# A fused transformer block: another order of work inside the two narrow attentions

## The reference, cut to what matters

```python
x = x + _L0_xattn_ref(_layernorm(x), ctx, ctx, ...)        # "a"
y = _layernorm(x)
# the second layer, "m":
x1 = rmsnorm(y, norm1_w)
q = x1 @ Wq.T
latent = layernorm(x1 @ Wdkv.T, ln_g, ln_b)                # 64 wide
k = latent @ Wuk.T
v = latent @ Wuv.T
q = apply_rope(q)
k = apply_rope(k)
scores = einsum('bhqd,bhkd->bhqk', q, k) / sqrt(8)         # causal
attn = softmax(where(causal, scores, -inf))
y = y + (attn @ v) @ Wo.T
```

## Time and profile before

| | us |
|---|---|
| median of three runs | 2048.15 (2042.94 to 2048.78) |
| the profiled execution's own time | 2049.34 |
| its span | 2047.5 |
| first attention, steady part (66 to 424 us) | 358 |
| second attention, steady part (470 to 986 us) | 516 |
| PE busy over the span | 1493.7 (73%) |
| DVE busy | 1348.0 (66%) |
| ACT busy | 1172.9 (57%) |
| POOL busy | 773.1 (38%) |

### The profile page before, as it was taken

The page is one execution under the profiler, slowest core; times in us unless marked ns, Lnnn a source line. Parts: engine busy times, 40 slices in busy tenths (PEclk is TensorE's granted clock), DMA queues, the critical chain, the costliest instruction groups (busy, mean ns, idle before and its releaser), DMA issues. The chain is left out here.

```text
span 2047.5 us, 63292 instructions
## 1 busy us (share of the span) xinstructions
PE 1493.7 (73%) x22193; PEld 1111.0 (54%) x22194; DVE 1348.0 (66%) x3733; ACT 1172.9 (57%) x2974; POOL 773.1 (38%) x823
## 2 busy tenths in 40 slices
PE   0688888846888877788424992888888884499991
PEld 0466666624555555556223780566666663377781
DVE  4577777636777777776454664678777875366665
ACT  2366666623544444444433990798888883377770
POOL 0000000022322323231485561336666666466661
PEclk9999999967999999999556995899999996699996
DMA  7110000000001000000012223000011111222227
GB/s 231 32 34 27 31 31 25 26 6 27 31 20 33 21 29 25 26 33 18 23 43 72 74 66 96 12 12 30 29 32 32 31 36 33 79 81 77 81 77 250
DMA packets 110889, 100.81 MB, mean 49 GB/s; under 512 B 17827, under 2 KB 98598, under 8 KB 110656
## 3 DMA queue, kind: packets, MB, share of 16 engines
q1 hardware_dynamic: 87648, 67.02, 11.0%
q0 software_dynamic: 12928, 25.60, 3.8%
q10 hardware_dynamic: 10080, 5.01, 0.8%
HBM read 43.25 MB, written 32.96 MB: 37 GB/s over the span
## 5 line engine op out<-in xcount | busy, mean ns | idle before, releaser
L2497 POOL DMA_INDIRECT e_back<-e_out_rows,e_G x142 | 148.4, 1045 | 98.8 <-issue 56.7
L664 DVE TENSOR_REDUCE m_mx<-m_pM 128x8 f32<-128x1024 f32 x128 | 155.6, 1216 | 29.6 <-PE m_pM L375 29.5
L1459 ACT ACTIVATE w_weights<-w_pS,w_ng 128x77 f32<-128x77 f32 x512 | 157.8, 339 | 17.7 <-DVE w_ng L1547 17.5
L526 ACT ACTIVATE m_PT<-m_pS 128x1024 f32<-128x1024 f32 x128 | 130.4, 1019 | 59.3 <-PE m_pS L404 58.0
L1112 POOL DMA_INDIRECT e_rows<-re_R,re_index x128 | 126.1, 985 | 63.7 <-issue 35.2
L526 ACT ACTIVATE a_PT<-a_pS 77x1024 f32<-77x1024 f32 x128 | 130.5, 1019 | 17.8 <-PE a_pS L404 12.6
L2520 DVE TENSOR_TENSOR e_gl<-e_g,e_gh 128x512 f16<-128x512 f32 x142 | 98.3, 692 | 57.4 <-ACT e_g L2464 53.7
L769 POOL TENSOR_SCALAR a_var<-a_aggr 128x4 f32<-128x4 f32 x16 | 3.1, 193 | 337.0 <-DVE a_aggr L590 337.0
L1660 POOL TENSOR_TENSOR w_weights<-w_weights,w_rec 128x616 f32<-128x616 f32 x64 | 77.9, 1217 | 125.4 <-DVE w_rec L1551 125.0
L664 DVE TENSOR_REDUCE a_mx<-a_pM 128x8 f32<-128x616 f32 x128 | 101.5, 793 | 33.0 <-PE a_pM L375 33.0
L1459 ACT ACTIVATION_READ_ACCUMULATOR w_weights<-w_pS,w_ng 128x1 f32 x512 | 113.6, 222 | 0.0
(11 more groups left out here) (383 smaller groups left out, 5651.1 us busy)
## 6 DMA issues: line engine op xcount, KB each, us to landing
e_G<-e_rows SPq DMA_DIRECT2D x106, 132.0 KB, 2.3
e_B<-e_back SPq DMA_DIRECT2D x16, 512.0 KB, 6.9
stage<-in_split SPq DMA_DIRECT2D x13, 512.0 KB, 4.6
Qs<-a_qh SPq DMA_DIRECT2D x128, 32.0 KB
Qs<-m_qh SPq DMA_DIRECT2D x128, 32.0 KB
Ks<-m_kh SPq DMA_DIRECT2D x32, 128.0 KB
e_R<-e_back SPq DMA_DIRECT2D x16, 256.0 KB, 3.5
w_stage<-in_late SPq DMA_DIRECT2D x16, 256.0 KB, 2.6
```

What stands on the lines that cost most here:

```text
L526: act.activation(PT[:NK, b % 2, 8 * half:8 * half + 8, :], pS[:NK, :, :], ACT.Exp, scale=float(1.0 / np.sqrt(HD))).then_inc(exp_done, 1)
L664: dve.tensor_reduce(out=mx[:, 8 * half:8 * half + 8], in_=pM[:, :, :NK], op=ALU.max, axis=AX.X).then_inc(m_max, 1)
L1459: ac = act.activation(weights[:, b % 2, n, :], pS[:, n // HB, n % HB, :KC], ACT.Exp, bias=ng[:, b % 2, n:n + 1], scale=float(WD) ** -0.5, ...
L2497: pool.indirect_dma_start(out=back, out_offset=bass.IndirectOffsetOnAxis(ap=G[:, r, s, D:D + 1].bitcast(I32), axis=0), in_=out_rows[:, r, ...
```

## The change

It moves instructions and hands some to another engine. No product, sum or copy is added or taken away, except that the high half of the latents is now made from PSUM and not from the copy in SBUF.

- `max_transpose` and `keep_max` of sequence b + 1 stand in the second half of step b, before `scores` of the second half. They stood at the start of step b + 1.
- The second half of the maxima stands right behind the first half of the scores, ahead of `project_output` and `values`.
- On DVE the maximum of the first half comes first in a step, ahead of the part in the slot.
- latT is made in slot 0 of step 0 for the next group. It was made in slot 1 of step 3 for the group after the next. q moves to a third slot (2) in the middle of step 0. ACT makes both of latT's outputs, `lh` and `lt`.
- The normalised latents (`latents`) are written behind the second maximum of step 3.
- The high half of the rotated q is made in step 1 and that of k in step 2, behind `output_hi`. They were made at the end of steps 0 and 1.
- The four scaled rows of the RMS norm (`rms_rows`) are made by ACT, ahead of the first `exps` of step 2. DVE made them.
- POOL makes the root for the squares ahead of ks in step 1.

```diff
-            order = ["q", "qs", "k", "ks", "v", "x", "lat", "latT"]
+            order = ["latT", "q", "qs", "k", "ks", "v", "x", "lat"]
...
-            slots = {(0, 0): "q", (0, 1): "qs", (1, 0): "k", (1, 1): "ks", (2, 0): "v", (2, 1): "x",
-                     (3, 0): "lat", (3, 1): "latT"}
+            slots = {(0, 0): "latT", (0, 2): "q", (0, 1): "qs", (1, 0): "k", (1, 1): "ks", (2, 0): "v", (2, 1): "x",
+                     (3, 0): "lat"}
...
@@ the step of PE
-                max_transpose(g, p, b)
-                what, gw, far = slot(b, 0, g, nxt, nxt2)
-                if what:
-                    project(what, gw, None)
+                if first and b in (0, GB - 1):
+                    project(first, ga, None)
                 if more:
                     maxima(pn, bn, 0, gn)
+                if first and b not in (0, GB - 1):
+                    project(first, ga, None)
                 if two:
                     turn_output(*two)
                 scores(g, p, b, 0)
+                if more:
+                    maxima(pn, bn, 1, gn)
+                if middle:
+                    project(middle, gm, None)
                 if two:
                     project_output(*two)
                 if before:
                     values(gp, pp, bp)
                 if more:
-                    maxima(pn, bn, 1, gn)
-                what, gw, far = slot(b, 1, g, nxt, nxt2)
-                if what:
-                    project(what, gw, None)
+                    max_transpose(gn, pn, bn)
+                if second:
+                    project(second, gb, None)
                 scores(g, p, b, 1)
@@ ACT
                 elif what == "latT":
-                    act.wait_ge(evac, u + 1)
-                    act.activation(lh[:], lt, ACT.Copy).then_inc(hi_made, 1)
+                    act.wait_ge(used, u + 1)
+                    wait(act, lat_lo, lin(g, 1, 0))
+                    settle(act, c)
+                    act.activation(lh[:], pP[:LAT, :TG], ACT.Identity, scale=SM("lg", LAT),
+                                   bias=SM("lb", LAT)).then_inc(hi_made, 1)
+                    act.activation(lt, pP[:LAT, :TG], ACT.Identity, scale=SM("lg", LAT),
+                                   bias=SM("lb", LAT)).then_inc(evac, 1)
...
                 if two:
                     output_hi(*two)
+                if b in (1, 2) and rotated:
+                    part(("qs", "ks")[b - 1], shift(g, 1), 1 - p)
+                if latent and b == 2 and nxt2:
+                    rms_rows(shift(g, 2))
                 exps(g, p, b, 0)
...
                 exps(g, p, b, 1)
-                if late:
-                    part(what, gw)
@@ the step of DVE
-                keep_max(g, b)
-                what, gw, far = slot(b, 0, g, nxt, nxt2)
-                if what:
-                    part(what, gw, (p + far) % 2)
+                if more:
+                    take_max(gn, bn, 0)
+                if first:
+                    part(first, ga, (p + far_a) % 2)
                 if two:
                     output_lo(*two)
                 if more:
-                    take_max(gn, bn, 0)
+                    take_max(gn, bn, 1)
+                    negate(gn, bn)
+                if first == "lat":
+                    latents(ga)
+                if middle:
+                    part(middle, gm, (p + far_m) % 2)
                 if two:
                     residual(*two)
                 if b == 0 and nxt2:
                     norm_stats(shift(g, 2))
                 if b == 1 and nxt2:
                     norm_rows(shift(g, 2))
-                if latent and b == 2 and nxt2:
-                    rms_rows(shift(g, 2))
                 if more:
-                    take_max(gn, bn, 1)
-                    negate(gn, bn)
-                what, gw, far = slot(b, 1, g, nxt, nxt2)
-                if what:
-                    part(what, gw, (p + far) % 2)
+                    keep_max(gn, bn)
+                if second:
+                    part(second, gb, (p + far_b) % 2)
                 if before:
                     divide(gp, bp)
@@ POOL
                 if b == 0 and nxt2:
                     rows(shift(g, 2))
-                for half_ in (0, 1):
+                for half_ in (0, 2, 1):
                     what, gw, far = slot(b, half_, g, nxt, nxt2)
+                    if b == 1 and half_ == 1 and nxt2:
+                        squares(shift(g, 2))
                     if what:
                         rope(what, gw)
-                if b == 1 and nxt2:
-                    squares(shift(g, 2))
```

More of the change, by code:

```diff
@@ L274, in slot @@
             what = slots.get((b, half))
-            if what in ("x", "lat", "latT"):
+            if what in ("x", "lat"):
                 return (what, shift(g, 2), 2) if nxt2 else (None, None, 0)
             return (what, shift(g, 1), 1) if what and nxt else (None, None, 0)
-        start_x = ["x", "lat", "latT"] if latent else ["x"]
-        start = ([(w, 0) for w in start_x] + [(w, 0) for w in order if w not in start_x]
-                 + [(w, 1) for w in start_x])
+        if latent:
+            start = [(w, 0) for w in ("x", "lat", "latT", "q", "qs", "k", "ks", "v")] + [("x", 1), ("lat", 1)]
+        else:
+            start = [("x", 0), ("q", 0), ("k", 0), ("v", 0), ("x", 1)]
         def earlier(g, b, by):
@@ L298, in hi_count @@
             per = [w for w in order if w in (("x", "qs", "ks", "latT") if latent else ("x", "q", "k"))]
-            lead = 2 if latent else 1
-            back = 1 if what in ("x", "latT") else 0
+            lead = 1
+            back = 1 if what == "x" else 0
             return lin(g, len(per), lead + per.index(what) + 1 - back * len(per))
@@ L489, in _, with part @@
         def _(act):
-            def part(what, g):
+            def part(what, g, p):
                 u = use(g, what)
@@ L520, in squares, with rms_rows @@
                                    accum_out=ms[:, b:b + 1]).then_inc(sq_done, 1)
+            def rms_rows(g):
+                act.wait_ge(ms_done, lin(g, 1, 1))
+                if not is_first(g):
+                    act.wait_ge(lat_lo, lin(g, 1, 0))
+                settle(act, c)
+                for b in range(GB):
+                    act.activation(xn[:, b:b + 1, :], Y[:, bass.ds(lin(g, GB, b), 1), :], ACT.Copy,
+                                   scale=rr[:, b:b + 1]).then_inc(rms_r, 1)
             def exps(g, p, b, half):
@@ L546, in begin @@
                 for what, k in start:
-                    if latent and what == "x" and k == 1:
-                        squares((None, 1))
-                    part(what, (None, k))
+                    if latent and what == "x":
+                        if k == 1:
+                            squares((None, 1))
+                        rms_rows((None, k))
+                    part(what, (None, k), k)
             def step(g, p, b, nxt, nxt2):
                 one, two = earlier(g, b, 1), earlier(g, b, 2)
-                what, gw, far = slot(b, 0, g, nxt, nxt2)
-                if what:
-                    part(what, gw)
+                first, ga, far_a = slot(b, 0, g, nxt, nxt2)
+                second, gb, far_b = slot(b, 1, g, nxt, nxt2)
+                rotated = latent and nxt
+                if first and (first == "latT" or not latent):
+                    part(first, ga, (p + far_a) % 2)
                 if two:
                     output_hi(*two)
+                if b in (1, 2) and rotated:
+                    part(("qs", "ks")[b - 1], shift(g, 1), 1 - p)
+                if latent and b == 2 and nxt2:
+                    rms_rows(shift(g, 2))
                 exps(g, p, b, 0)
@@ L562, in step @@
                     squares(shift(g, 2))
-                what, gw, far = slot(b, 1, g, nxt, nxt2)
-                late = what in ("qs", "ks")
-                if what and not late:
-                    part(what, gw)
+                if second in ("x", "k"):
+                    part(second, gb, (p + far_b) % 2)
                 exps(g, p, b, 1)
-                if late:
-                    part(what, gw)
             def finish():
```

44 lines of the change are left out of this document (20 added, 24 removed).

## The result

The changed kernel took 2061.39 us (median of five runs, 2055.79 to 2061.8), the kernel before, on the same chip, 2046.42 (2038.59 to 2048.78). The ratio is 1.0075, with a 95% interval of 1.0056 to 1.0094: slower by 0.75%, 15 us. In the profiled executions the span grew from 2047.5 to 2059.9 us, by 12.4.

What follows compares the result with a forecast made beforehand. In the second attention no engine but the loop through the copies was taken to bound. The terms -9.1 + 12.6 - 1.3 - 1.0 + 1.0 = +2.2 us took 2048.15 to 2050.5 us, range 2030 to 2068.

Steps and rivals of the forecast that it cites:

- `a`: First attention: a transpose and moved maxima save 0.65 us a group over fourteen groups, -9.1 us (-3 to -17).
- the opening of `m`: Start of the second attention: it loses latT of the second group and its copy on DVE, about -1.3 us.
- The loop through the copies: Second attention: chain from one group's first `maxima` to the next, 31.04 us against 30.14; +12.6 us over fourteen groups.
- `maxima` to `turn_heads`: Second attention, step 3: half of the maxima and latT leave, a transpose comes; 6.46 to 5.47 us, 0.99 won.
- `turn_heads` to the low half of q: Second attention: sum for q queues on POOL behind root and latents' low half; 11.07 to 12.96 us, 1.89 lost.
- copies: Second attention: SP's fifteen copies and their landing stay at 12.61 us a group.
- The step that failed: Second attention: groups longer than 30.14 us, through PE's falling clock or the hardware loop's turns, were taken as they are.
- The last stretch: Second attention, last group: PE waits for `ng` in bare steps, about 0.26 us a step, +1.0 us.
- Slack in the loop: Rival, second attention: POOL reaches q's sum by 9.6 us, engines' steps bind at 29.6 a group; 2030 us; chance 0.20.
- Late k: Rival, second attention: ACT's squares slip 2 us, each group pays 0.9 to 1.2 us more; 2066 us; chance 0.12.
- The waiting transpose: Rival, first attention: `scores` and `turn_heads` queue behind the transpose, 0.3 us over 64 steps, +19, 2069 us; chance 0.13.
- PE's clock, 0.10 of the chances: Rival about the clock of PE, its text cut from the prediction; chance 0.10, with 0.05 counted as slower.

Runs made afterwards that it cites:

- Experiment 3: Changed kernel, loop kept, with POOL making the root for the rows behind both halves of q in step 0: 2037.75 us, 0.997.
- experiments 2: Kernel before, with the second attention's sixteen groups written out so its hardware loop never turns: 2030.2 us, 0.9937.
- 4: First attention as changed, second attention as in the kernel before: 2040.16 us, 0.9975.
- experiments 1: Changed kernel, with the second attention's sixteen groups written out so its hardware loop never turns: 2039.25 us, 0.9975.
- 8: Changed kernel with the four scaled rows of the RMS norm back on DVE: 2060.28 us, 1.0076.
- 10: Kernel before, with POOL making the root for the rows behind both low halves of step 0: 2061.29 us, 1.008.
- experiment 11: Kernel before with the late root on POOL, plus DVE's normalised rows of step 1 moved behind `ng`, in both attentions: 2087.7 us, 1.0192.
- experiment 12: Experiment 3's kernel with `turn_heads` ahead of the second half of the scores on PE in step 3 of the second attention: 2049.73 us, 1.0046.
- experiment 6: Experiment 3's kernel with the first maxima ahead of latT on PE in step 0 of the second attention: 2038.36 us, 0.9975.
- 7: Experiment 3's kernel with four groups in place of two in the second attention's hardware loop, so it turns once: 2022.73 us, 0.9904.

## Why the prediction was right, and where it was not

The time, 2061.4, lies within the range and 11 us above the forecast of 2050.5. It is none of the rivals: the sum's mechanisms are there, with prices left out. The range is 38 us wide, and its width is part of why it holds. The forecast was a change of 2 us, and its largest chance, 0.42, stood on no change that can be told; what came, slower by 15 us, had 0.34.

Against the sum (+2.2) the profiled span grew by 12.4. The 10.2 between them are +3.9 in `a`, +4.4 in the opening of `m`, +3.1 in its fourteen groups, and -1.2 in all the rest. That the fourteen groups are so near is partly luck, as the table below shows: one part was 5.4 better than forecast, another 7.4 worse.

*The loop through the copies.* Near in all three parts of an undisturbed group (5.74, 12.85 and 12.44 against 5.47, 12.96 and 12.61); the sum, 31.03 against 31.04, is closer than its parts, whose errors cancel. Experiment 3 shows the cause. Over the fourteen groups between the first `maxima` that waits for copies (500.87 us before, 499.65 after) and the last, the three parts changed by +14.7 us together:

| part | predicted | measured |
|---|---|---|
| `maxima` to `turn_heads` | -13.9 | -19.3 |
| `turn_heads` to the low half of q | +26.5 | +33.9 |
| copies | 0 | +0.1 |

(The prediction takes off another 1.0 for the last of the fourteen, which has no root ahead.) The first was undersized because the group that was followed, with 6.46 us, was one of the quick ones of before: the mean was 7.36, and up to 9.56 at a granted clock of 0.66. After the change it is 5.99. In the second, nine ordinary groups lost 2.06 us each (1.89 forecast), the last lost 0.67, and the four turned groups lost 3.66 each.

*The step that failed* is "Other groups take longer than 30.14 because PE's clock falls or because the hardware loop turns; I take both as they are." A turned group cost 3.05 us more than its neighbours in this part before, and 4.65 after. The stand of PE at a turn (2.37 to 2.83 us before, 2.94 to 3.49 after) lies on the loop through the copies, and so does the clock of 0.50 behind it. Of the +17.9 us of `m`, 8.8 is there in the written-out pair as well, where the sum had 11.3; the other 9.1 came with the turns, and the sum had nothing for them.

*The opening of `m`.* I forecast -1.3; from the start of `m` to the first `maxima` that waits for copies it was +3.1. The order of before takes 73.1 to 75.0 us for this stretch in experiments 2 and 4 and in the kernel before, the changed order 74.8 to 76.3 in experiments 1 and 8 and in the changed kernel, so the size is uncertain and only the sign is told. One wait of 3.79 us for the latents went, but one of 3.86 came, in which the second mask product waits for DVE's maximum, and k waits 1.75 us for the low half of the latents. The last stretch, behind the fourteen groups, had +1.0 in the sum and changed by 0.1.

*`a`.* The groups are right: from 290.19 to 333.22 the two take 43.03, 21.5 each.

```profile
290.19 5.79 SPq L320 DMA_DIRECT2D Qs<-a_qh  x8
311.61 5.77 SPq L320 DMA_DIRECT2D Qs<-a_qh  x8
333.22 5.79 SPq L320 DMA_DIRECT2D Qs<-a_qh  x8
```

The count was wrong. Before, the first groups of `a` took 20.85 to 21.58 us and only nine took 22.1; I had carried to fourteen. Nine times 0.6 is 5.4.

*The rivals.* Slack in the loop: fell. The sum for q is done 10.74 us after `turn_heads` (forecast 10.98, the rival 9.6), and PE waits for the copies in every group. Experiment 3 brings the early sum that this rival asked for (done after 9.0 us) and groups of 29.7 to 30.2 where the rival had 29.6; but PE waits for the copies before every group even there, so that the rival's other half, that the engines' own steps then set the pace, is not shown. The time was 2037.75 us, where the rival had 2030. Late k: not seen in the changed kernel. Away from turns the copies take 12.4 to 12.9 us (13.2 in the last group). In two of the turned groups they took 14.5 and 14.4, and in the same two of before 15.3 and 13.4; what lengthened them stays open, but it was not k, since SP's queue waited for the low half of k only once from 470 to 986 us, for 0.3 us:

```profile
SPq L83 <- POOL m_kl L824: 0.3, 1, 0.3
```

The waiting transpose in `a`: 2.4 us in three waits. PE's clock, 0.10 of the chances: not in the stage's mean, 0.94 after 0.93, but at the turns. All four stands of the changed kernel (2.94 to 3.49 us) were followed by a clock of 0.50, within 0.6 us of PE's return. Of the four of before, one of 2.70 us was, 1.5 us behind the return, and three, of 2.37, 2.39 and 2.83 us, were followed by 1.00. Nor is the changed order needed: in experiments 4 and 10, which have PE's order of before in `m`, stands of 2.36 to 2.90 us were followed by a clock of 0.50, at seven of eight turns at once and at the eighth 1.6 us behind the return, and in experiment 11 at two of four (2.37 and 2.94 us; not behind 2.34 and 2.43). What such a stretch costs a group by itself no run shows; a mask product took 0.61 us at 0.50 and 0.39 at 1.00. Why the clock falls at some turns and not at others stays open.

*Why the stand is longer.* The rows show transfers on a queue that the profile calls instruction; that PE stands for them is a reading of their times, and no run shows it. These transfers, in 10 us around a turn of the changed kernel (from 798 us on; a digit is 0.25 us):

```profile
DMA  0000020000000002000000000002000000000000
...
q8 instruction: 3, 0.05, 1.9%
```

and of the kernel before (from 855 us on):

```profile
DMA  0000000000030000000020000000000020000000
...
q8 instruction: 3, 0.05, 2.0%
```

The second transfer is at 801.75 and, in a finer view, 860.1; PE returns at 804.37 and 862.60, 2.6 and 2.5 us behind it. But PE had ended at 801.43 in the changed kernel, 0.3 ahead of the transfer, and at 860.23 in the other, 0.1 behind it. It is so at all eight turns: the return is 2.5 to 3.0 us behind the transfer in either kernel (mean 2.7), and the transfer 0.3 to 0.6 us behind PE's last work in the changed kernel and 0.1 ahead of it before. So from that transfer to PE's return it is nearly the same time in both, and the stand is 0.7 us longer on average (3.23 and 2.57). In kernel 2, which has no turns in `m`, such transfers come 6.5 to 12.5 us apart from 470 to 960 us, and no stand of this kind goes with them. Why the transfer comes later against PE's work stays open: my one idea on it, the place of `turn_heads`, fell in experiment 12, and that of the body's first instruction in experiment 6.

## What to carry over

The pace of one quiet group, 31.04 us forecast and 31.03 found, did not hold for the stage, whose turned groups took 36.3 to 36.6: count the groups of each kind, and cost what a change does to the disturbed ones when it moves work onto the chain that sets the pace. In an engine's queue, put first what the next engine on that chain waits for: moving 1.3 us of root behind the sum for q gave back the change's loss (from 1.0075 to 0.997), and the same edit was a loss in the kernel before (1.008), where DVE had to wait for that root ahead of a maximum. An order is good only together with the orders of the engines around it.

## What was not expected of the hardware

At each turn of the hardware loop of `m` that the profiles hold, PE stood with nothing named but issue. With the transpose of the maxima first behind the turn (the kernel before, kernels 4, 10 and 11) it was 2.34 to 2.94 us, with latT first (the changed kernel, 3 and 8) 2.94 to 3.49, and 2.88 to 4.06 in kernel 12, with the maxima first (6) 3.01 to 3.51. With four groups in the body (7) the one stand was 3.50 us. In kernel 3 the four turned groups, with the clock of 0.50 behind their stands, took 34.89 to 35.58 us, and all others behind the opening 29.66 to 30.18. Writing the sixteen groups out brought 0.6% in the kernel before and 1.0% in the changed one.

In `a`, whose loop turns as often, no such stand shows. In the kernel before, two of its groups (250.5 to 294.8 us) hold 710 records of products on PE, and two of `m` (732.92 to 798.64) hold 865. In 175 us of the loop of `a` (205 to 380 us of the kernel before) the instruction queues move nothing, and the queue of the first line below is the only one with packets; in as many us of the loop of `m` (675 to 850) they move 24 packets, as the second line has it (queue: packets, MB, share of the 16 engines):

```profile
q1 hardware_dynamic: 7256, 5.01, 9.1%
```

```profile
q8 instruction: 24, 0.39, 1.0%
```

So of these two stretches the one with packets on the instruction queue has the stands, and the one with none has none; but kernel 2 has 54 packets on that queue from 470 to 960 us and no stand. Whether PE waits at a turn for what that queue moves was not shown, nor whether the length of the body has a part in it: no run varies the length of the body of `a`.
